# Mixtures of experts: the weights' loads are issued in the routing block, not in the normalization's block

## The reference

```python
x = x + mamba(layernorm(x));     x = x + mixture0(layernorm(x))
x = x + rotary(layernorm(x));    x = x + mixture0(layernorm(x))
x = x + sinks(layernorm(x));     x = x + mixture1(layernorm(x))
x = x + latent(layernorm(x));    x = x + mixture1(layernorm(x))
```

## Time and profile before

| | us |
|---|---|
| median of 3 runs | 4134.72 |
| lowest and highest run | 4134.48, 4136.27 |
| profiled execution, its own time | 4140.78 |
| span of the profiled execution | 4138.2 |

### The profile page before, as it was taken

How to read it: one execution, slowest core, us unless ns; L and a number is a source line. 1 busy time by engine, 2 the same in 40 slices (tenths; PEclk the granted TensorE clock), 3 DMA queues, 4 the chain that set the end, 5 groups by cost and what they waited for, 6 DMA issues and landing times. The chain is left out here.

```text
span 4138.2 us, 68603 instructions
## 1 busy us (share of the span) xinstructions
PE 3287.4 (79%) x19706; PEld 2595.8 (63%) x19707; DVE 2811.4 (68%) x6227; ACT 2274.7 (55%) x5958; POOL 1809.1 (44%) x3103
## 2 busy tenths in 40 slices
PE   7799958916888499089999999999737399999374
PEld 3355546715777377068778878788635288888253
DVE  5699956636777566468768778588553388888542
ACT  3599913405777244078768678688302266666021
POOL 0299923567663144636446356255237200000265
PEclk9799978958999599589999999999856699999566
DMA  2011132430000335300000000000234300000524
GB/s 84 20 48 49 49 144 89 136 101 13 1 1 1 144 114 131 113 29 19 17 11 20 14 14 19 11 17 20 112 86 67 102 1 1 1 1 1 180 51 105
DMA packets 133309, 221.35 MB, mean 53 GB/s; under 512 B 28912, under 2 KB 106608, under 8 KB 131264
## 3 DMA queue, kind: packets, MB, share of 16 engines
q1 hardware_dynamic: 99216, 147.84, 10.7%
q0 software_dynamic: 33792, 69.83, 7.4%
HBM read 162.60 MB, written 54.80 MB: 53 GB/s over the span
## 5 line engine op out<-in xcount | busy, mean ns | idle before, releaser
L1271 POOL DMA_INDIRECT ex_xr<-scratch_rows,mo_token x288 | 287.5, 998 | 324.8 <-issue 289.1
L596 POOL TENSOR_TENSOR sc_h<-sc_h,sc_c 128x512 f32<-128x512 f32 x256 | 327.2, 1292 | 198.1 <-DVE sc_h L633 190.2
L3044 DVE TENSOR_TENSOR sa_pT<-bank,sa_pT 128x512 fp32r<-128x512 f32 x512 | 329.9, 686 | 34.4 <-ACT sa_pT L2912 30.5
L2904 ACT ACTIVATE sa_p<-bank,sa_nm 128x512 f32<-128x512 f32 x512 | 346.9, 689 | 2.5 <-DVE sa_nm L3035 2.5
L633 DVE TENSOR_TENSOR_SCAN sc_h<-sc_da,bank 128x512 f32<-128x512 f32 x256 | 311.1, 1220 | 38.4 <-ACT sc_da L576 23.5
L2733 PE MATMUL bank<-sa_kT,sa_qT 128*128 128x512 f32 x1024 | 332.7, 436 | 1.5 <-DVE residual L3011 1.5
L3031 DVE TENSOR_REDUCE sa_mx<-bank 128x2 f32<-128x1024 f32 x256 | 312.4, 1220 | 25.6 <-PE bank L2735 21.7
L1337 PE MATMUL bank<-mo_w_gu,ex_xT 128*128 (+2 forms) x1152 | 315.0, 402 | 1.1 <-issue 0.6
L2757 PE MATMUL bank<-sa_pT,sa_v 128*128 128x256 f32 x2048 | 301.4, 290 | 17.1 <-DVE sa_pT L3044 16.4
L2757 PEld LDWEIGHTS bank<-sa_pT,sa_v 128*128 128x128 f32 x2048 | 260.2, 190 | 40.0 <-DVE sa_pT L3044 31.4
L2912 ACT ACTIVATE sa_pT<-bank 128x512 fp32r<-128x512 f32 x512 | 274.3, 585 | 7.7 <-PE bank L2745 0.5
(11 more groups left out here) (402 smaller groups left out, 9458.5 us busy)
## 6 DMA issues: line engine op xcount, KB each, us to landing
scratch_ys<-ex_yo SPq DMA_DIRECT2D x192, 128.0 KB
mo_w_gu<-in_w_gu SPq DMA_DIRECT2D x2, 9216.0 KB, 26.2
sc_c<-scratch_c SPq DMA_DIRECT2D x64, 256.0 KB, 3.1
sa_share<-scratch_shares SPq DMA_DIRECT2D x256, 64.0 KB, 2.6
mo_w_dn<-in_w_dn SPq DMA_DIRECT2D x2, 4608.0 KB, 47.5
mo_w_dn<-in_w_dn SPq DMA_DIRECT2D x2, 4096.0 KB, 34.7
scratch_rows<-ln_stage POOLq DMA_DIRECT2D x64, 128.0 KB, 21.9
ex_xr<-scratch_rows,mo_token POOLq DMA_INDIRECT x288
```

The lines of the kernel that those rows point to most:

```text
L596: pool.tensor_tensor(h, h, C[u], ALU.mult).then_inc(used.sem, 1)
L1271: pool.indirect_dma_start(xr[u][:, :], None, rows, bass.IndirectOffsetOnAxis(ap=token[:, i:i + 1], axis=0), bounds_check=rows.shape[0] - 1 ...
L2904: act.activation(pr[h][:, :], SC[2 * s_ + h][:, :], ACT.Exp, bias=nm[:, col:col + 1], scale=SCALE, accum_out=rs[:, col:col + 1]).then_inc( ...
L3044: dve.tensor_tensor(spot(1), PT[h][:, :].rearrange("p (k n) -> p k n", k=TPB), spot(0).bitcast(F32), ALU.subtract).then_inc(*inc("kept_d"))
```

## The change

`late_loads` is no longer called by SyncE at the end of its list in the normalization's block, but as its first step in the routing's block, ahead of its waits there. The transfers, their sizes, their order and their queue stay the same, and so do all waits on them. `layer_norm` loses the parameter.

```diff
@@ layer_norm
-            if loads is not None or late_loads is not None:
+            if loads is not None:
                 @block.sync
                 def _(sp):
-                    if loads is not None:
-                        loads(sp)
+                    loads(sp)
                     if not c.fills:
                         zero_scratch(c, sp)
-                    if late_loads is not None:
-                        late_loads(sp)
@@ moe, call of layer_norm
                 layer_norm(c, xnT, loads=loads if which == 0 else None, products=logits,
-                           last_step=add_bias, rows=(rows, rowed), late_loads=late_loads)
+                           last_step=add_bias, rows=(rows, rowed))
@@ moe, routing's block
                 @block.sync
                 def _(sp):
+                    late_loads(sp)
                     if which == 0:
                         sp.wait_ge(bsplit.sem, bsplit.at(5))
```

More of the change, by code:

```diff
@@ L152, in _, with layer_norm @@
             sp.wait_ge(stored.sem, 16)
-def layer_norm(c, xnT, loads=None, products=None, last_step=None, rows=None, late_loads=None):
+def layer_norm(c, xnT, loads=None, products=None, last_step=None, rows=None):
     nc = c.nc
```

## The result

| | before | after |
|---|---|---|
| median, us | 4135.5 (4 runs) | 4072.93 (4 runs, 4070.81 to 4074.93) |
| span of the profiled execution | 4138.2 | 4076.2 |
| ratio after/before | | 0.9846, interval 0.9829 to 0.9863 |

The kernel became 62.6 us faster, 1.5%; forecast were 4074.4 us and a gain of 60.3. The code lost three lines ahead of the blocks and gained one, so lines of after are 2 or 3 lower: the normalization's block is L174 still, the routing's is L860, its first VectorE operation L965, the row stores are L187, the tags store is L955.

What follows compares the result with a forecast made beforehand. No engine was busy throughout; the bound was 62.3 us of all-engine standstill at GpSimd's drain after normalization. Less 2.0 us for four block changes, 60.3 us off 4134.7 gives 4074.4 us, range 4069 to 4085.

Steps and rivals of the forecast that it cites:

- What ends the block: Normalization's block: GpSimd's drain, waiting for row stores delayed beside the loads, ends last; VectorE idles 62.3 us over four blocks.
- What is late next: Normalization's block after the change: GpSimd through near 583.5 and 3867.5, so VectorE ends last, at 591.2 and 3873.95.
- What holds the stores: Normalization's block: DMA engines alternate queues packet by packet; 1 KB store rows wait behind long weight packets, over 30 us.
- The sum: Whole kernel: 62.3 us idle less 2.0 for four block changes saves 60.3; 4134.7 falls to 4074.4 us.
- the price of a block change: Boundary after VectorE's last operation: 0.5 us taken for each of four; saving's ends 59.9 and 61.1 us.
- The drain's tail: GpSimd's drain in the normalization's block: 0.082 us for each DMA since the last drain, 1.3 us for 16.
- First kind, loads beside the routing: Routing's block, mixtures without the copy: weights land at head + 34.8, bias stores by + 38; margin 12 us, cost nothing.
- Second kind, the narrow place: Routing's block, mixtures with the copy: tags land + 55.3, block ends + 56.5; cost 0, bounds 0 and 2.6 us each.
- The half rate of the down weights: Weight loads in the second kind: 213 GB/s, where the first load had 433; kept unchanged in the forecast.
- No slowdown of the routing's operations: Routing's block: load traffic doesn't lengthen its operations; value 0, bounds 0 and 4 us if all four blocks were 2% slower.
- The rule against the change: Skill's advice to issue a DMA early and wait late: issuing some 31 us later gives up cover.

## Why the prediction was right, step by step

- *What ends the block.* Right: GpSimd's drain, held by row stores behind the weights. Moving the weights alone gives all of it, the copy next to nothing, and short packets free the stores with the loads still in place.
- *What is late next.* Right: VectorE. GpSimd's drain ends 6.8 us before it in the fourth mixture, at block + 24.6; I had put it at + 24.9 (3867.5). That close agreement is luck: the last store landed later than forecast there and the tail was shorter. In the first mixture it was + 23.4, forecast + 25.5.
- *What holds the stores.* Right, by the run with short pieces, that they wait their turn behind long packets. A detail was off: they don't move in rows of 1 KB, with a turn for each. The DMA view of before (the window of the earlier trace rows) has 512 packets between 2 and 8 KB, and the 16 stores are 2.1 MB, so a packet of a store is 4 KB, four rows:

```profile
DMA packets 3217, 18.37 MB, mean 317 GB/s; under 512 B 304, under 2 KB 2352, under 8 KB 2864
```

- *The sum.* 60.3 forecast, 61.0 in the blocks, 62.6 in the medians. The term that was mis-sized is the price of a block change: 0.5 us taken, 0.3 measured (1.3 for 4), at my other end. Of the rest, 0.8 us is that the median before is now 4135.5 and not 4134.72; the last 0.8 is less than runs of one kernel differ.
- *The drain's tail.* Growing with the number of software DMAs was right, the value was not: 1.3 us taken, 0.7 measured, and it did no harm. The price of the earlier trace rows doesn't carry over. Counted from the last landing, the drains after the change are 8.2 us after 96 gathers and scatters, 3.5 us after 64 gathers (part of the 5.3 us was the last gather's landing) and 0.70 us after 16 stores, which is 0.085, 0.055 and 0.044 us for each. Why it differs by form stays open.
- *First kind, loads beside the routing.* Right in the outcome: SyncE is past its six bias stores 35.6 to 36.1 us after the head, of 50.8; forecast + 38. But the queue does not finish its transfers one after another, as the prediction read out of two landings: in the first mixture the down weights, issued at 588.7, landed at 623.4, and five of the six bias stores issued behind them had landed by then, the first at 620.7. (DMA view of after, the windows in which they are issued; the first bias store was issued at 595.6.)

```profile
mo_w_dn<-in_w_dn SPq DMA_DIRECT2D x1, 4096.0 KB, 34.6
...
mo_b_gu<-mo_bpart SPq DMA_DIRECT2D x1, 16.0 KB, 25.1
```

- *Second kind, the narrow place.* Right in its order and its outcome. Forecast + 55.3 for the tags against VectorE's + 56.5, measured + 54.1. The copy, forecast at + 53.8, landed at + 52.6. Of these 1.2 us the weights ahead of it gave 0.7 (+ 47.4 against + 48.1) and the copy 0.5 (5.2 us behind the weights, where I had taken 5.7). The tags came 1.5 us behind the copy, as forecast, and the margin is 2.2 us instead of 1.2.
- *The half rate of the down weights.* Kept, and so it was: 197 GB/s from 3864 to 3872 after the change, with no row stores about. In pieces of 1 KB it is 204 GB/s (3858 to 3862 of that run), so the packets' length isn't its cause. It goes to 96 partitions instead of 128; whether this is the cause was not tested.
- *No slowdown of the routing's operations.* Right: the large comparison, now wholly beside the weights, takes 6552 ns as in the earlier trace rows, at full DMA share in the window from 3844:

```profile
3844.00:3848.00 4.00, 0.00 (x0) 0.00 (x0) 3.86 (x5) 0.00 (x0) 4.00 (x4) 0.50 1.02 442
```

- *The rule against the change.* Issuing late did give up cover (Trainium skill, DMA: Bandwidth & Descriptors, Rules for kernel authors), and by the distance from SyncE's branch to VectorE's drain 35.8 us of cover turned into 2.2 in the second kind and 38 into 14 in the first, but none of it reached the path. The run that issues early within the same block, but behind the stores, shows that the rule and this change don't exclude each other.

## What to carry to other kernels

When all engines stand still at a block's end, ask which drain or wait ends last and what its transfers compete with: small stores that something waits for should not be in flight together with long-packet loads that nobody needs yet. Order them, stores first, rather than pushing the loads far away; that gave the same 4073 us here and kept 9.6 us of cover instead of 2.2. After such a move, look at what now stands behind the loads in the same queue, and price the margin by adding a transfer of known length.

## What the runs showed of the hardware that I had not expected

- SyncE's issue is no fixed price, and pieces count more than bytes: the tags store's issue lasted 0.37 us with an empty queue, 0.37 us behind 14 MB of weights in long pieces, and 30.3 us when the 2 MB copy in 1 KB pieces stood between. A second such copy right behind the first stood in its own issue for 45.6 us. With the weights in 1 KB pieces SyncE stood in issues for 49.5 us of a 50.0 us block.
- Transfers of one hardware queue can land out of order: stores of 16 KB landed up to 2.7 us before a 4 MB load that was issued 6.9 us ahead of the first of them.
- A software DMA of 128 KB to DRAM takes 2.1 us with no load beside it (median of 64 stores), and took 21.9 us beside long-packet loads and 5.1 us beside the same bytes in 1 KB packets.
- GpSimd's closing drain waits for its own software DMAs and ends 0.70 us after the last of 16 stores has landed, 1.35 us after the last of 32; SyncE's drain took 0.12 us with 14 MB of its loads in flight.
